# Expert rounds in teams of two groups in a one-core graph kernel: state logits made with each team, bias parts on 128 partitions

## What is computed

```
h = x @ W_in + b_in
for l in range(3):
    agg    = segment_sum(h[src], dst) / deg
    logits = concat([h, agg]) @ router_W[l] + router_b[l]      # 8 experts
    gates  = softmax of the top 2 logits, 0 elsewhere
    weak   = relu(agg @ weak_W[l] + weak_b[l])                 # 4 experts, 256 wide
    sh     = relu(agg @ strong_W1[l] + strong_b1[l])           # 4 experts, 512 wide
    strong = sh @ strong_W2[l] + strong_b2[l]
    conf   = sigmoid(h @ conf_W[l] + conf_b[l])
    h      = h + conf * sum_e gates[e] * experts[e]
x = layernorm(x + h @ W_out + b_out)
x = layernorm(x + gat(elu(gat(x))))
```

## Time and profile before

| | us |
|---|---|
| median of 3 runs | 5852.51 |
| lowest and highest run | 5852.5, 5859.92 |
| the profiled execution | 5857.3 |
| its span, first to last instruction | 5855.7 |
| up to the first gather of round 0 | 329.67 |
| round 0, to the first gather of round 1 | 1108.2 |
| round 1, to the first gather of round 2 | 1104.1 |
| round 2, to the first gather of attention | 1179.4 |

### The profile page before, as it was taken

One profiled execution on the slowest core, in us unless ns is written; L12 is line 12 of the kernel. 1 busy time (PEld: TensorE's weight loads), 2 busy tenths in 40 slices (PEclk: granted clock), 3 DMA queues, 4 the chain that ended last, 5 costly groups with the idle time before them and its releaser, 6 DMA issues.

```text
span 5855.7 us, 59691 instructions
## 1 busy us (share of the span) xinstructions
PE 3218.5 (55%) x11995; PEld 2032.2 (35%) x11995; DVE 3452.8 (59%) x6754; ACT 1199.8 (20%) x2737; POOL 4188.6 (72%) x4323
## 2 busy tenths in 40 slices
PE   4068889999879899989899999200000000000000
PEld 3055555556545555565465566200000000000000
DVE  5337667674556666636566665555555556556563
ACT  1022223333223233323233333200000000000000
POOL 7777777772777777547777766477777767777777
PEclk8569999999889999979999999655555555555555
DMA  4144443441443333333333332223222222222221
GB/s 111 51 147 109 112 112 106 111 110 50 141 111 112 108 111 110 87 107 104 102 102 100 102 95 70 54 59 60 59 60 59 59 46 56 55 55 55 56 55 50
DMA packets 248524, 500.35 MB, mean 85 GB/s; under 512 B 103196, under 2 KB 132437, under 8 KB 248037
## 3 DMA queue, kind: packets, MB, share of 16 engines
q0 software_dynamic: 176592, 446.04, 29.5%
q1 hardware_dynamic: 55226, 33.55, 2.2%
q10 hardware_dynamic: 16608, 19.67, 1.0%
HBM read 464.23 MB, written 34.72 MB: 85 GB/s over the span
## 4 chain that ended last, share of the span: by engine, by line
POOL 25%; PE 24%; issue 15%; DVE 13%; DVEq 12%; DMA 6%; ACT 2%; ACTq 0%; POOLq 0%; SPq 0%
POOL ring L589 22%; PE ps_w1a L1677 5%; PE ps_w1b L1677 4%; PE ps_gate L1702 4%; PE ps_wide L1702 3%; DMA ring<-gat_tab,stage 3%; DVE ps_wide L1135 3%; PE ps_weak_a L1689 2%; PE ps_weak_b L1689 2%; DMA ring<-hidden_tab,stage 2%; DVEq L1167 2%; DVEq L883 1%; DVE ps_wide L930 1%; DVEq L1177 1%; DVEq L1180 1%
## 5 line engine op out<-in xcount | busy, mean ns | idle before, releaser
L589 POOL DMA_INDIRECT ring<-hidden_tab,stage x2400 | 2304.8, 960 | 954.4 <-issue 891.1
L589 POOL DMA_INDIRECT ring<-gat_tab,stage x1600 | 1543.6, 965 | 585.9 <-issue 545.1
L886 DVE TENSOR_TENSOR ps_wide<-ps_wide,ring 128x1024 f32<-128x1024 f32 x450 | 560.2, 1245 | 208.7 <-SPq L415 124.6
L1677 PE MATMUL ps_w1a<-agg_team_t,wbuf 128*128 128x512 f32 (+1 forms) x1248 | 562.2, 573 | 7.3 <-ACT strong L1343 5.9
L1702 PE MATMUL ps_gate<-wbuf,strong 128*128 128x256 f32 x2400 | 560.0, 380 | 0.0
L1677 PE MATMUL ps_w1b<-agg_team_t,wbuf 128*128 128x512 f32 (+1 forms) x1248 | 556.1, 568 | 0.0
L1807 PE MATMUL ps_w1a<-ident,agg_team_t 128*128 128x128 f32 x28 | 7.8, 434 | 995.9 <-DVE agg_team_t L1213 995.9
L1702 PE MATMUL ps_wide<-wbuf,strong 128*128 128x256 f32 x2304 | 537.3, 380 | 0.0
L1702 PEld LDWEIGHTS ps_gate<-wbuf,strong 128*128 128x128 f32 x2400 | 433.3, 191 | 110.6 <-issue 47.7
L1702 PEld LDWEIGHTS ps_wide<-wbuf,strong 128*128 128x128 f32 x2304 | 416.0, 191 | 77.9
L1495 ACT ACTIVATE ps_gate<-shifted 128x36 f32<-128x36 f32 x296 | 60.4, 204 | 1862.4 <-DVEq L1124 1849.1
(11 more groups left out here) (356 smaller groups left out, 4578.3 us busy)
## 6 DMA issues: line engine op xcount, KB each, us to landing
ring<-hidden_tab,stage POOLq DMA_INDIRECT x2400, 2.8
ring<-gat_tab,stage POOLq DMA_INDIRECT x1600, 2.6
hidden_tab<-h_res ACTq DMA_DIRECT2D x24, 512.0 KB, 3.0
hidden_tab<-h_res SPq DMA_DIRECT2D x12, 512.0 KB, 8.5
wbuf<-in_L_gnn_strong_W SPq DMA_DIRECT2D x6, 1024.0 KB, 9.5
wbuf<-in_L_gnn_strong_W SPq DMA_DIRECT2D x12, 512.0 KB, 14.3
gat_tab<-h_res ACTq DMA_DIRECT2D x7, 476.0 KB, 3.7
gat_tab<-h_res ACTq DMA_DIRECT2D x12, 272.0 KB, 2.4
```

Of the source, the lines that this page charges most:

```text
L589: return pool.indirect_dma_start(out=ring[:, b, 0:width], out_offset=None, in_=table, in_offset=bass.IndirectOffsetOnAxis(ap=stage[:, half ...
L886: nc.vector.tensor_tensor(wide_s, wide_s, rows(u), ALU.add).then_inc(ring_free, 1)
L1677: last = mm(ps_w1[c % 2][:, 0:size * P], w1_w[:, k, s, c * P:(c + 1) * P], agg_team_t[:, k, 0:size * P], start=k == 0, stop=k == 1)
```

## The change

- `TEAM` becomes 2: 24 teams and one last single group, 25 steps a round. The batches of other work (states, residuals, the rows of x) stay at 4 under the name `BATCH`.
- A strong expert's first layer for two groups fills one PSUM bank with two chunks of 256 columns (`PAIRS` = 2), and its second layer fills one bank with both groups; the banks alternate by expert. All four experts have hidden rooms of their own (`strong_room`).
- TensorE's step: `second` of experts 2 and 3 of team q-1 around `turn_agg`, the router straight into nodes by logits (no turning back), first layers 0 and 1, weak experts of group 0, first layers 2 and 3, second layers 0 and 1, turning of team q-1's state, weak experts of group 1, projection.
- VectorE's step: sum of the next team's first group, the late additions of team q-1 (one weak, two strong), ranks, gates, sum of the second group, then one weak and two strong additions.
- ScalarE's exponential stands behind all relus of the step.
- The own logits are made before round 0 only, as soon as chunks of states have arrived. In rounds 0 and 1 the finished team's state is turned and multiplied by the next round's router (`state_logits`) in the place where round 2 projects.
- Of the single last group in round 2 state, turning and projection come inside the round.
- The bias parts of experts are made on 128 partitions, 24 columns each for weak and strong, ahead of the sort, and go through `parts_tab` in 6 DMAs to their rows. 14 more small parameter loads (`rt_bias` per group of a batch).
- The compaction is VectorE's alone, 49 iterations with a drain each.

In the order of instructions, ScalarE in the middle of the program, a team's step before: `ex` is the exponential, `strong` the relus, `weak` and `x_res` the scaling by gates.

The core of the diff:

```diff
-TEAM = 4
+BATCHES = -(-GROUPS // BATCH)
+TEAM = 2
 TEAMS = GROUPS // TEAM
-BATCHES = TEAMS + 1
+TURNS = TEAMS + 1
+PAIRS = 2
...
+            par(bias_all[:, 0, :], weak_b.rearrange("l e n -> (l e n)").rearrange("(p k) -> p k", p=P))
+            par(bias_all[:, 1, :], strong_b2.rearrange("l e n -> (l e n)").rearrange("(p k) -> p k", p=P))
...
+            nc.vector.tensor_copy(bias_parts_all[:, 0, :, :], bias_all[:])
+            for nth in range(1, len(PART_ROWS)):
+                dve.drain()
+                nc.vector.tensor_tensor(bias_all[:], bias_all[:], bias_parts_all[:, nth - 1, :, :], ALU.subtract)
+                dve.drain()
+                nc.vector.tensor_copy(bias_parts_all[:, nth, :, :], bias_all[:])
+            dve.drain().then_inc(s_parts, 1)
...
-            bias_parts(bias_f, wk_parts[:].rearrange("p l n -> p (l n)"))
-            dve.drain().then_inc(s_weak_parts, 1)
-            bias_parts(bias_s, strong_parts)
-            dve.drain().then_inc(s_parts, 1)
...
+            with dve.Fori(0, GROUPS) as g:
                 at = dve.value_load(cum_at[0:1, bass.ds(g, 1)], min_val=0, max_val=COLS - RUN)
-                dve.wait_ge(s_compact, g + 1)
...
+                dve.drain()
...
                     gather_next(0)
                     if after == 1:
                         fill_up(r)
                     if tail:
-                        add_strong(r, q - 1, NS - 1, TEAM)
+                        add_weak(r, q - 1, TEAM - 1, TEAM)
+                        add_strong(r, q - 1, 2, TEAM)
+                        add_strong(r, q - 1, 3, TEAM)
                     rank_experts(r, q, size)
                     weigh_experts(r, q, size)
+                    between(2 if size == 1 else 0)
+                    gather_next(1)
                     add_weak(r, q, 0, size)
...
+                def step(q, size, tail=True):
+                    relus = (q + r * TURNS) * (NS * PAIRS) + NS * PAIRS
                     if tail:
-                        second(r, q - 1, TEAM, NS - 1)
+                        second(r, q - 1, TEAM, 2)
                     turn_agg(r, q, size)
+                    if tail:
+                        second(r, q - 1, TEAM, 3)
                     router(r, q, size)
                     strong_first(r, q, size, 0)
-                    turn_logits(r, q, size)
+                    strong_first(r, q, size, 1)
                     weak_experts(r, q, size, 0)
...
+                    strong_first(r, q, size, 2)
+                    strong_first(r, q, size, 3)
+                    second(r, q, size, 0)
+                    second(r, q, size, 1)
+                    if tail:
+                        turn_state(r, q - 1, TEAM, relus - 1)
+                    if size > 1:
+                        weak_experts(r, q, size, 1)
+                    if tail:
+                        project(r, q - 1, TEAM, relus)
```

More of the change, by code:

```diff
@@ L71 @@
 EARLY_X = 6
-EARLY = (TEAMS - 1) * TEAM
+EARLY = (BATCHES - 2) * BATCH
 LOWEST = -1.5e38
@@ L1018, in gather_next, with between @@
                                 done.then_inc(agg_ready, 1)
-                    def between():
-                        if r == LAYERS - 1 and spare:
-                            residual(spare.pop(0))
+                    def between(count):
+                        if r == LAYERS - 1:
+                            for _ in range(min(count, len(spare))):
+                                residual(spare.pop(0))
                     spare = list(meanwhile)
@@ new lines, in relu @@
+                w(act, w2_ready, n * NS + (s + 1 - NS))
+                for pair in range(PAIRS):
+                    act.wait_ge(w1_ready, n * (NS * PAIRS) + (s * PAIRS + pair + 1))
+                    for half in range(2):
+                        c = 2 * pair + half
+                        k = (r * NS + s) * 4 + c
+                        last = nc.scalar.activation(strong[s][:, c, 0:size * P], ps_w1[pair][:, half * TEAM * P:half * TEAM * P + size * P], ACT.Relu, bias=b1_t[:, k:k + 1])
+                    last.then_inc(relu_ready, 1)
@@ L1391, in _ @@
             for r in range(LAYERS):
-                def step(q, size, after, tail=True):
+                def step(q, size, tail=True):
                     if tail:
-                        scale_strong(r, q - 1, TEAM, NS - 1)
-                    for k in range(2):
-                        take_agg_t(r, q, size, k)
-                    logits_t(r, q, size)
-                    relu(r, q, size, 0)
+                        scale_strong(r, q - 1, TEAM, 2)
+                    take_agg_t(r, q, size)
+                    if tail:
+                        scale_strong(r, q - 1, TEAM, 3)
@@ L1399, in step @@
                     logits(r, q, size)
-                    relu(r, q, size, 1)
+                    for s in range(NS):
+                        relu(r, q, size, s)
                     gate_exp(r, q, size)
@@ L1434, in _ @@
-                step(TEAMS - 1, TEAM, 1)
-                step(TEAMS, 1, 0)
-                scale_strong(r, TEAMS, 1, NS - 1)
+                    if tail:
+                        take_projected(r, q - 1, TEAM)
+                if r == 0:
+                    act.wait_ge(s_dummy, 16 * (LAYERS + 5))
+                    own_copy(0)
+                    for q in range(BATCHES):
+                        if q + 1 < BATCHES:
+                            own_copy(q + 1)
+                        own_take(q)
+                    act.wait_ge(s_long, 1)
@@ L1775, in batch_operand @@
+                pe.wait_ge(s_wts, 16 * WT_DMAS * (r + 1))
+                step(0, TEAM, False)
+                with pe.Fori(1, TEAMS) as q:
+                    step(q, TEAM)
+                step(TEAMS, 1)
+                second(r, TEAMS, 1, 2)
+                second(r, TEAMS, 1, 3)
+                turn_state(r, TEAMS, 1, (r + 1) * TURNS * NS * PAIRS)
+                project(r, TEAMS, 1, (r + 1) * TURNS * NS * PAIRS)
             def batch_operand(b):
```

413 lines of the change are left out of this document (181 added, 232 removed).

## The result

The changed kernel takes **5874.58 us** (median of 7 runs, 5872.3 to 5877.07) against 5855.27 for the kernel before (7 runs): ratio **1.0033**, 95% interval 1.0023 to 1.0043. The profiled execution took 5872.3, with a span of 5870.7, 15.0 longer than before.

The account below looks back on a forecast made before the run. GpSimd's gather feed plus the last teams' tail bounds a round. Preamble -2.6, rounds 0 and 1 +2 each, round 2 -4.5 sum to -3.1: 5857.3 becomes 5854.2, the median 4.8 below, so 5850 us; range 5838 to 5862.

Parts of the forecast that it names:

- What bounds a round: Expert rounds: GpSimd's gathers plus what the last teams need set the length; TensorE's 39.4 us step keeps under the feed's 41.5.
- Tails: After a round's last gather: a team of two and the odd group take 62 us instead of 91, gaining 29.
- Start of a round: First team: TensorE waits for weights until +65.5, first unit of group 3 freed at +94, GpSimd loses 20 us.
- Middle: Later steps: loop of 38.8 us hides under TensorE's 39.4; heavy groups cost the feed some 11 us, last gather at +1048.
- rival B: Middle steps: exponential behind all relus makes the gates' loop the bound; steps of 41 us, +40, 5890 us; chance 0.23.
- Sum of rounds 0 and 1: Gathers plus tail, 1048 + 62 = 1110 us: +2 in each round, the tail's gain eaten by the feed.
- Preamble: Before the first gather: bias parts save 29.3 us, compaction grows from 33 to 70; first gather at 327.1, -2.6.
- Rival E: Preamble's bias parts: only the casts' 21.0 us go, first gather 8.3 later than forecast, 5858 us; chance 0.05.
- Rival D: Preamble: L522 gathers are slow for another reason, 29.3 us stay, compaction costs all the same, +26.7, 5876; chance 0.03.
- Round 2: Last expert round: last sum at +1063, variances at +1133 instead of +1135, z's wait of 2.7 us gone: -4.5.
- A1: Expert rounds: the feed loses only the start's 20 us, the ring carries heavy groups; -33, 5817 us; chance 0.18.
- A2: Round starts: VectorE isn't stopped, as when weights land or the ring drains sooner; -82, 5768 us; chance 0.09.

Follow-up runs that it names:

- the control: The kernel before (teams of four) with the weight loads issued ahead of the passing on of the first ring: 5863.13 us, ratio 1.0018.

## Why the prediction was wrong

**What bounds a round: right.** Gathers plus tail is what every run followed. The steps of TensorE were 39.4 us where nothing held them (40.1 in round 2, with the projection), as forecast from the earlier trace rows. There luck had a part: the terms listed add up to 39.5, not to 38.8, so the 0.6 "with gaps" made good a slip.

**Tails: right.** 62 forecast, 62.1 and 63.1 measured.

**Start of a round: right in mechanism, place and nearly in size.** Forecast: weights +64.6, turn +65.5, unit freed +94, GpSimd loses 20 us from 74 on. Measured: turn +64.6, gather resumed at +94.9, halt 23.4 to 23.8 us from +71.3. Wrong was only that the first turn waits for the weights "in both kernels": in the kernel before it waits for VectorE's sums until +68.8 (the control's first line). That the halving of the team makes the weights the bound was thus not seen, though the time of the turn was. The 74 took 5.08 us a unit; free of waits it is 4 x 1.25 = 5.0, and 57 gathers make 71.3. This moved the halt's start, not its end, and so cost nothing.

**Middle: the term that was mis-sized, 11 us where 17 to 18 came.** The start's 20 us were 22.2 and 22.5 in rounds 0 and 1 (23.4 and 23.7 less the 1.25 between any two gathers). The later loss, forecast 11, was the rest of the 40.6 and 39.1 us by which the gathers grew: 18 and 17. It stands as pauses of 4.4, 2.7, 4.6, 4.5, 4.1 and 4.5 us in round 1, and some 30 more are 0.3 to 0.5 us above the usual distance. The last gather is at +1053 to +1057, not +1048. Against it, TensorE's idle spell at the eight-unit group is 20.8 us, not 16. The table's own parts leave 3 us open: 1048 is 34 above 1014, and 20 + 11 are 31.

What the later loss hangs on is shown by the exponential's experiment: with it behind expert 1 the later loss of round 1 falls from 17 to 4 us. The prediction put the loop through the gates at 38.8 us against 39.4 and called the exponential's place rival B, "0.6 us added to the loop's 38.8". That is the step that failed: the loop was read with a mean group of four units, and the groups differ. With one of five units it is 38.8 + 1.57, above 40, and 15 of the 49 groups have five or more. The turns of TensorE in the changed kernel, round 1, show it in two steps whose second group has five units:

```profile
2408.20 0.60 PE L1647 MATMUL ps_w1a<-ident,x_res 128*128 128x128 f32 x4
...
2448.25 0.66 PE L1647 MATMUL ps_w1a<-ident,x_res 128*128 128x128 f32 x4 [0.53 <-DVE x_res L905]
...
2489.54 0.66 PE L1647 MATMUL ps_w1a<-ident,x_res 128*128 128x128 f32 x4 [1.71 <-DVE x_res L905]
```

TensorE waits there for VectorE's second sum, and the steps are 40.0 and 41.3 us. Of the 24 steps of round 1 the five with such a second group take 40.0 to 41.3, those with smaller groups 39.4 (the first 38.6), and with the exponential behind expert 1 all of these take 39.2 to 39.4. From the first turn to the odd group's it is 17.7 us less there: 5.0 in those five steps, 12.8 in the steps around the groups of six to eight units and the last team, which were 47.5 + 65.7, 57.8, 49.0 and 46.4 and become 39.4 + 69.5, 55.3, 46.5 and 42.9. So B came in part. 18 of 24 steps stay below 41, but VectorE's wait for the exponential in round 1 is 6.1, 7.5 and 6.4 us in the step behind the groups of eight, seven and six units, and above 6 was what B named as its sign. Of the 65 us that the exponential's place costs, the forecast had the first step's part in its 20; for the rest it had no term.

**Sum of rounds 0 and 1: a slip.** 1048 + 62 = 1110 is 2 above round 0's 1108.2, but 6 above round 1's 1104.1; the text wrote +2 for each. So 4 of the 18 us between forecast and result are arithmetic. The others are 6.4 in the preamble and 9 and 6 in the gathers and tails of rounds 0 and 1, less 4.2 in round 2 and 3.0 in attention.

**Preamble: -2.6 forecast, +3.8 measured.** The bias part went as read. The L522 gathers (now L530) end 28.7 us earlier, and none takes longer beside the former place of the bias parts (the one of 6.86 us lies ahead of it, at 90, and was there before too):

```profile
L530 POOL DMA_INDIRECT wbuf<-in_src,wbuf x49: 940/944/6862, 80.0 to 146.0; - x49
...
152.82 1.00 POOL L538 DMA_INDIRECT meta_tab<-wbuf,weak  x1 [5.88 <-issue]
```

But the scatter behind them now starts after 5.88 us of pause; before it was 2.25. The program makes GpSimd wait there until the last of these gathers has landed. That one landed 2.4 us after its start before (at 177.08), and 6.0 us after it now (at 152.03), and the scatter starts 0.8 us behind in both. The DMA engines' busy share is 0.91 from 140 to 152 us now, and was 0.13 from 167 to 177: issued earlier, the last gathers fall into a busier time. So the metadata chain moved by 25.1, not 29.3: the step from GpSimd's saving to the chain's was taken as whole. The compaction's iteration, 1.43 forecast, is 1.46 in its steady part, and up to 1.64 at its start:

```profile
324.85 0.20 DVE L849 TENSOR_SCALAR wbuf<-wbuf  x1 [1.25 <-issue]
326.31 0.20 DVE L849 TENSOR_SCALAR wbuf<-wbuf  x1 [1.26 <-issue]
```

71.4 us in all to SyncE's store, 39.7 more than the 31.7 of both engines in turn, where I subtracted 33 and had 37. So the first gather is late by 4.2 for the metadata and 2.7 for the compaction, and 0.5 came back behind them.

Rival E is not borne out either. The Trainium skill, "SBUF — State Buffer", section "Who interferes with whom", says that copies, casts and tensor_scalars can hold the port pair that VectorE shares with GpSimd, and that a tensor_tensor takes only its read side, which writing descriptors does not need (the Trainium skill calls this inferred). By it 12 x 1.75 = 21.0 us would go here. The traces do not agree: L522's whole stretch shrank from 96.2 (79.4 to 174.7 and 0.94) to 66.9 us, by 29.3, more than the casts. And in the kernel before a gather that starts inside a tensor_tensor does not end there:

```profile
127.85 3.35 DVE L685 TENSOR_TENSOR ring<-ring,wk_parts 1x3072 f32<-1x3072 f32 x1
...
128.90 4.24 POOL L522 DMA_INDIRECT wbuf<-in_src,wbuf  x1 [0.31 <-issue]
```

It needs 0.94 and had 2.30 us of the tensor_tensor left, but ends at 133.14, 0.12 us behind the cast that follows (131.27 and 1.75). So the tensor_tensor held it too. Rival D's price, 5876, was 3 too low besides: 29.3 more than the forecast's 5850 is 5879.

**Round 2: -8.7 instead of -4.5.** Last sum at 3631.95, +1063.2, as forecast (+1063); variances at 3700.99, +1132.3 (forecast +1133). From there to the first attention gather 38.4 us, before 44.3: I counted 2.7 of z not waited for, and it was 5.9.

```profile
3631.95 0.35 DVE L905 TENSOR_SCALAR x_res<-part,rdeg 128x256 f32<-128x256 f32 x1
...
3700.99 0.19 DVE L1002 TENSOR_SCALAR ln_r<-ln_mv 128x44 f32<-128x44 f32 x1
```

**The rivals.** A1 and A2 (the feed loses less) did not come by themselves. A2's place, however, was right: it says "as when weights land or the ring drains sooner". With the weights and the exponential put right, the kernel gives 5776, near A2's 5768. The two edits together take 27 to 36 us from each round of the changed kernel. B's time, 5890, was nearer to the result than the forecast, its cause half right. The attention rounds' -3.0 was taken as 0; in the nine traces at usual speed this part lasts from 2129.4 to 2134.3 us.

## What to carry to other kernels

When a pipeline's steps are made smaller, read again what the first step waits for: a load that was hidden behind the first large batch (here weights at +64.6 behind sums at +68.8) becomes the bound when the first batch is half as large, and a full ring behind it hands the delay to the producer for the rest of the loop. Issue such loads first. And where gates or control values close a loop with a margin under 2% on the mean, work the loop out with the largest common item, not with the mean one: placing a 0.2 us exponential two relu groups later cost 65 us of 5800.

## What the runs showed of the hardware

- The same program took 5855 us on some chips and 8168 and 8179 on two others, with pauses of 5 to 7 us marked "issue" at branches of the instruction streams. There the order of kernels changed too: the exponential's edit, 0.9925 elsewhere, was 1.035. Its cause was not looked for.
- Taking 18 one-partition VectorE operations (41.24 us busy, 21.0 of it casts) from beside GpSimd's gathers took 29.3 us from the gathers' stretch. A gather that began inside an fp32 tensor_tensor took 4.24 us instead of 0.94 and ended with the cast behind it.
- 3.6 of these 29.3 us came back at once: the last gather took 6.0 us to land instead of 2.4, while the DMA engines' busy share was 0.91 instead of 0.13. In the seven kernels with that edit at usual speed the wait for it was 2.8 to 6.7 us. Which transfers were in its way was not followed up.
